# Turning h and K through DRAM in a two-layer graph kernel: h's blocks by two stores and eight fetches, K's by one store and four, with a rearranged loop, start and end

## The chip, the cores and the metric

The kernel runs on one core of one Trainium2 chip (trn2). The metric is the device time of one execution in microseconds (us). The kernel before took 1233.65 us in the median of 3 runs (1232.67 to 1234.98). All tensors are float32.

## The reference, cut to what is computed

x is 128 matrices of 128 rows (graph nodes) by 512 features; adj is one 128x128 matrix of zeros and ones with a full diagonal. Each of the 128 matrices is worked on alone.

```python
h = relu(layernorm(x))
z_l, z_g, v = h @ W_lang.T, h @ W_grav.T, h @ W_V.T
zn = z_l / norm(z_l)                        # row norms
A_l = max(zn @ zn.T, 0) * not_eye           # 128 x 128
d2  = max(sq + sq.T - 2 * z_g @ z_g.T, 0)
A_g = exp(-d2 / (2 * sigma**2)) * not_eye
K = w_l * row_normalised(A_l * adj) + (1 - w_l) * row_normalised(A_g * adj)
x = x + (K @ v) @ W_O.T                     # layer 0
h = relu(layernorm(x))
x = x + (adj * adj).T @ h + bias            # layer 1
```

## The kernel before, in words

**Tiles.** Four matrices (GB) form a group, and 32 groups (NG) pass through a software pipeline of 32 iterations. A slot of `x_ring` holds one group's x, [128 rows, 4 matrices, 512]. float32 products are made of three passes of a split pair (`passes`, line 183): every operand X is kept as X_hi (a copy by ACT, rounded to the PE's format) and X_lo = X - X_hi (by DVE, `lo`, line 586). So each result in PSUM costs an ACT copy and then a DVE subtraction before the bank is free.

**Weights folded at the start.** W_lang and W_grav are squared into lower block triangles `Lw`, W_V and W_O into `MT`. Then h Lw h^T gives one triangle's half of a symmetric matrix, called P here, and P + P^T is the full one. The turn of P, a transpose of [128,128] per matrix, is made of a DVE transpose of 32x32 blocks (`turn_p`, line 775) and transfers that move the blocks across partitions through DRAM (`store_p` 223, `fetch_p` 227). `sum_s` (line 784) adds P and its turned form.

**One iteration i on PE** (line 978): eight `y_block` products of group i (60 matmuls of 512 columns) into the ring of five PSUM banks; the 96 matmuls of 256 columns into `p_ps` (line 998), with the four transposes of K of group i-1 between them (`transposes_K`, line 954, into `kt_ps`); `k_v` of group i-1 for four matrices (12 matmuls); the product v of group i (48 matmuls); `layer1` of group i-2 (12 matmuls). PE takes a ring bank only when `drained` has counted its last reader (`free`, line 931).

**The others.** ACT (line 433) copies y_hi, h2_hi, K^T_hi (`kt_copy`, 527, from `kt_ps`), P, v_hi, and hT_hi of the next group out of `h_turned` (`turned_hi`, 427), and computes exponentials, norms' outputs and h2. DVE (line 702) makes the lo parts, statistics, masks, `combine` (the last step of K), residual sums (`add` 658, `output` 689), and turns the 32x32 blocks of h in place (`turn_blocks`, 602). POOL makes h2_lo, adds the bias, and computes in this order: the factors of the second layernorm of group i-1 (`norm2`, 336, which needs all four `stats` of DVE), `row_norms` of i (345), `norm1` of i+2, `mask_norms` of i.

**SP's queue** (line 249) takes all transfers in a written order: load x of i+2, the 16 transfers of `turn_h` (243) that move each 32x32 block column of h to its partitions within SBUF, then P's first store, the store of the row norms (it waits for POOL's `row_norms`), P's second store, four fetches, the spread of the norms, four fetches, four stores of the output.

**Order that matters below.** On DVE: ... y_lo 5, y_lo 6, `combine`, blocks of h, y_lo 7, y_lo 8, blocks of h, `kt_lo`, four x statistics, then adds and statistics of group i-1 with the last `stats` before most of the squared norms of i, then v_lo, hT_lo and `turn_p`. On ACT: `kt_copy` before the two copies of P; then per matrix b: v_hi, hT_hi, with h2 of matrix 0 (`h2_full`, 494) placed behind hT_hi of b = 2, ahead of v_hi of b = 3. PE's next `y_block` waits for all four hT_lo (line 980).

Of the kernel before, what the change touches and what calls it, by code (L numbers as in the profile page):

```python
# [5 lines left out]
ALU = mybir.AluOpType  # L6
# [14 lines left out]
def gnn_pair(nc, x, adj, w_lang, w_grav, w_v, w_o, gate_logit, log_sigma, bias, out):  # L21
# [12 lines left out]
    TURN = 16 * NQ * NQ  # L34
    assert C == NQ

# [19 lines left out]
    with ExitStack() as ctx:  # L56
# [65 lines left out]

        p_dram = [nc.dram_tensor(f"p_dram_{l}", [P, NQ, GB * Q], F32).ap() for l in range(2)]
# [47 lines left out]
        blocks_ready, turned = sem("blocks_ready"), sem("turned")  # L171
        p_blocks = sem("p_blocks")
        p_stored, p_turned = [[sem(f"p_{what}_{l}") for l in range(2)] for what in ("stored", "turned")]
        ht_hi, ht_lo = sem("ht_hi"), sem("ht_lo")
        ln2_last = sem("ln2_last")
# [4 lines left out]
        x2b_last = sem("x2b_last")  # L180
# [14 lines left out]
        def h_blocks(i, j):  # L195
            return h[i * Q:(i + 1) * Q, j].rearrange("p b c q -> p (b c q)")

        def turned_to(i, j):
            return h_turned[j * Q:(j + 1) * Q, i].rearrange("p b c q -> p (b c q)")
# [3 lines left out]

        def x_rows(g, b):

            return x_ring[:, bass.ds(g % SLOTS, 1), b].rearrange("p s d -> p (s d)")

# [4 lines left out]
        def _(sp):  # L212
# [3 lines left out]

            def store_out(g, use):
                for b in range(GB):
                    sp.wait_ge(drained, use + b + 1)
                    sp.dma_start(out_g[bass.ds(g, 1), b].rearrange("g n d -> (g n) d"),  # L220
                                 x_rows(g, b)).then_inc(out_stored, 16)
# [21 lines left out]
            def turn_h(g):  # L243
                sp.wait_ge(blocks_ready, GB * g)
                for i in range(NQ):
                    for j in range(NQ):
                        sp.dma_start(turned_to(i, j), h_blocks(i, j)).then_inc(turned, 16)  # L247
# [33 lines left out]
            iteration(NG - 2, load=False)  # L281
            use = first_use(NG - 1) + PER - GB
            store_out(NG - 3, use)
            store_out(NG - 2, use + 2 * GB)
            store_out(NG - 1, use + 3 * GB)
# [4 lines left out]
        def _(pool):  # L290
# [61 lines left out]
            def iteration(i, before=True, lag=True, after=True, x_next=True):  # L352
# [10 lines left out]
                if before and not after:  # L363
# [14 lines left out]
            for b in range(GB):  # L378
                h2_lo(NG - 2, b)
            g = NG - 1  # L380

            def last_factors(q):
# [3 lines left out]
                pool.tensor_tensor(ln2[:, RSTD, b0:b1], ln2[:, VAR, b0:b1], neg_half[:, b0:b1], ALU.pow)\  # L386
                    .then_inc(ln2_rstd, 1)
                pool.wait_ge(ln2_rstd, 2 * q + 1)
                pool.tensor_tensor(ln2[:, SHIFT, b0:b1], ln2[:, NEG_MEAN, b0:b1], ln2[:, RSTD, b0:b1], ALU.mult)\
# [3 lines left out]
            for b in range(GB // 2):  # L393
                add_bias(g, b)
            last_factors(1)
            for b in range(GB // 2, GB):
                add_bias(g, b)


        @block.scalar  # L400
        def _(act):
# [5 lines left out]
            def normalize(g, b0):  # L407
                if b0 == 0:
# [3 lines left out]
                    elif not isinstance(g, int) or g > 1:  # L412
                        act.wait_ge(turned, TURN * (g - 1))
# [13 lines left out]
            def turned_hi(g, b):  # L427
                if b == 0:
                    act.wait_ge(turned, TURN * g)
# [3 lines left out]
            def iteration(i, before=True, lag=True, after=True):  # L433
# [30 lines left out]
                if not after:  # L464
                    shift(i)
                for c in range(C):
                    if not before:
                        act.wait_ge(setup_mm, 3 * C + c + 1)
                        act.activation(MT[0][:, c], bank(n), ACT.Copy).then_inc(hi_ready, 1)
                    n += 1  # L470
                if before:
                    act.wait_ge(kv_done, GB * i)
                for b in range(GB):
                    if not after and b == 1:
                        exponentials(i)
                    act.wait_ge(v_done, GB * i + b + 1)
                    act.activation(v[0][:, b], bank(n), ACT.Copy).then_inc(hi_ready, 1)  # L477
                    n += 1
                    if after:
                        turned_hi(i + 1, b)  # L480
                    if not after and b == GB - 2:
# [3 lines left out]
                    if before and after:  # L485
                        for k in {0: [], 1: [], 2: [0], 3: [1, 2, 3]}[b]:
# [7 lines left out]
            def h2_full(g, b, last=False):  # L494
# [4 lines left out]
                if b == 0:  # L499
                    wait_for(act, h2_split, GB * g)  # L500
                act.activation(h2f[:, b], x_rows(g, b), ACT.Relu, bias=ln2[:, SHIFT, b:b + 1],  # L501
                               scale=ln2[:, RSTD, b:b + 1]).then_inc(h2_done, 1)

            def h2_copy(g, b):
                act.wait_ge(h2_done, GB * g + b + 1)
                if b == 0:
# [13 lines left out]
            def w_g_K_g(g):  # L520
                act.wait_ge(deg_step, 5 * g + 5)
                wait_for(act, kt_done, g)
# [4 lines left out]
            def kt_copy(g):  # L527
                act.wait_ge(kt_done, g + 1)
                wait_for(act, kv_done, GB * g)
                act.activation(KT[0][:, :, :], kt_ps[:, :, :], ACT.Copy).then_inc(kt_hi, 1)  # L530
# [32 lines left out]
            lw_hi(1, side, side_hi, 2, C)  # L563
            for b in range(GB):
                t_hi(b, SETUP + b)
            act.wait_ge(a2_step, 1)
# [9 lines left out]
            for b in range(GB):  # L576
                h2_full(NG - 1, b, last=True)
                h2_copy(NG - 1, b)
# [3 lines left out]
        def _(dve):  # L582
# [70 lines left out]

            def kt_lo(g):
                dve.wait_ge(kt_hi, g + 1)
                dve.tensor_tensor(KT[1][:, :, :], kt_ps[:, :, :], part(KT[0][:, :, :]), ALU.subtract).then_inc(kt_split, 1)
# [8 lines left out]
            def last_factors(b0, b1, before):  # L665

                t = [ln2[:, n, b0:b1] for n in range(LN_STEPS)]
                m0, m1, q0, q1 = (bn2[:, b0:b1, n] for n in (1, 4, 2, 5))
# [435 lines left out]
```

## Time and profile before

| | |
|---|---|
| median of 3 runs | 1233.65 us (1232.67 to 1234.98) |
| the profiled execution, and its span | 1233.85 us, span 1232.1 us |
| mean granted TensorE clock | 0.992 |
| PE / DVE / ACT / POOL busy | 97% / 86% / 58% / 50% |
| chain that ended last | PE 93%, DVE 3%, ACT 1%, SP's queue 1% |
| DMA | mean 118 GB/s; SP's queue 38% of 16 engines |

```profile
PE   7989999999999999999999999999999999999994
DVE  5667888899888889888888988888898888899878
PEclk9999999999999999999999999999999999999998
h_turned<-h SPq DMA_DIRECT2D x496, 64.0 KB, 2.0
```

Each digit is the busy share of one fortieth of the span (30.8 us) in tenths; PEclk is the granted clock likewise. A matmul record ends where a model puts it, so starts are the safer numbers. A line such as "x496, 64.0 KB, 2.0" is a kind of transfer, its count, its size and the median us from issue to landing.

### The profile page before, as it was taken

How to read it: one execution, taken by the hardware profiler on the slowest of the kernel's cores; microseconds unless marked ns; L12 is line 12 of the kernel's file. 1: busy time of each engine (PE TensorE's matmuls, PEld its weight loads, DVE VectorE, ACT ScalarE, POOL GpSimd, SP SyncE). 2: the span in 40 equal slices, each digit the busy share in tenths (PEclk: the TensorE clock that was granted, in tenths of full speed). 3: DMA queues.
4: the chain of work that ended last, by engine and by line, in shares of the span. 5: the costliest groups of instructions: out<-in, count | busy, mean ns of one | idle time of the engine just before them, and what ended most of it. 6: DMA issues, size and time to landing. Idle time of an engine off the chain costs nothing.

```text
span 1232.1 us, 22833 instructions
## 1 busy us (share of the span) xinstructions
PE 1199.0 (97%) x6076; PEld 1023.3 (83%) x6076; DVE 1062.1 (86%) x1892; ACT 714.5 (58%) x1324; POOL 610.9 (50%) x991
## 2 busy tenths in 40 slices
PE   7989999999999999999999999999999999999994
PEld 7777888888888888888888888888888888888882
DVE  5667888899888889888888988888898888899878
ACT  5344655665565566556566655556665555665543
POOL 1203554545655444665454466545456554545545
PEclk9999999999999999999999999999999999999998
DMA  7122234344333444433343443344443334443302
GB/s 267 52 77 77 75 113 136 127 128 145 111 96 118 140 128 132 138 117 95 120 136 128 136 121 118 102 126 133 127 141 113 108 112 135 129 126 111 111 1 103
DMA packets 115457, 145.10 MB, mean 118 GB/s; under 512 B 20848, under 2 KB 52720, under 8 KB 115440
## 3 DMA queue, kind: packets, MB, share of 16 engines
q1 hardware_dynamic: 114864, 144.57, 38.4%
q10 hardware_dynamic: 576, 0.33, 0.1%
q8 instruction: 7, 0.11, 0.0%
q14 instruction: 10, 0.08, 0.0%
HBM read 62.46 MB, written 49.87 MB: 91 GB/s over the span
## 4 chain that ended last, share of the span: by engine, by line
PE 93%; DVE 3%; ACT 1%; SPq 1%; issue 1%; DMA 0%; POOL 0%; DVEq 0%; POOLq 0%
PE ring L944 76%; PE p_ps L998 14%; PE kt_ps L957 1%; PE ring L1042 1%; SPq L247 1%; DMA x_ring<-in_L_gnn_W_lang 0%; ACT h2f L501 0%; DVE bn L663 0%; DVE x_ring L698 0%; ACT h L419 0%; DVE chain L802 0%; PE ring L1051 0%; DVE v_lo L589 0%; DVE x_ring L660 0%; DVE ln L676 0%
## 5 line engine op out<-in xcount | busy, mean ns | idle before, releaser
L342 POOL TENSOR_TENSOR h_lo<-h2f,h_hi 128x512 fp32r<-128x512 f32 x124 | 156.7, 1292 | 323.3 <-ACT h_hi L508 323.1
L944 PE MATMUL ring<-hT_hi,Lw_hi 128*128 128x512 f32 x640 | 250.5, 391 | 7.5 <-DVE hT_lo L609 4.3
L944 PE MATMUL ring<-hT_hi,Lw_lo 128*128 128x512 f32 x640 | 250.4, 391 | 0.0
L944 PE MATMUL ring<-hT_lo,Lw_hi 128*128 128x512 f32 x640 | 250.4, 391 | 0.0
L589 DVE TENSOR_TENSOR y_lo<-ring,y_hi 128x512 fp32r<-128x512 f32 x256 | 169.7, 682 | 46.8 <-ACT y_hi L440 46.5
L944 PE MATMUL ring<-MT_hi,hT_hi 128*128 128x512 f32 x512 | 199.4, 389 | 1.4 <-DVE MT_lo L589 1.4
L944 PE MATMUL ring<-MT_hi,hT_lo 128*128 128x512 f32 x512 | 199.2, 389 | 0.0
L944 PE MATMUL ring<-MT_lo,hT_hi 128*128 128x512 f32 x512 | 199.2, 389 | 0.0
L440 ACT ACTIVATE y_hi<-ring 128x512 fp32r<-128x512 f32 x256 | 152.2, 597 | 79.1 <-PE ring L944 75.1
L477 ACT ACTIVATE v_hi<-ring 128x512 fp32r<-128x512 f32 x128 | 76.0, 594 | 190.1 <-PE ring L944 190.1
L327 POOL TENSOR_TENSOR x_ring<-x_ring,bias_sb 128x512 f32 (+1 forms) x124 | 157.8, 1304 | 1.9 <-ACT h2f L501 1.9
L944 PEld LDWEIGHTS ring<-hT_hi,Lw_hi 128*128 128x128 f32 x640 | 121.0, 189 | 34.1 <-DVE h_lo L870 2.8
L998 PE MATMUL p_ps<-y_hi,hT_hi 128*128 128x256 f32 x512 | 147.1, 287 | 0.0
L998 PE MATMUL p_ps<-y_hi,hT_lo 128*128 128x256 f32 x512 | 145.0, 283 | 0.0
L998 PE MATMUL p_ps<-y_lo,hT_hi 128*128 128x256 f32 x512 | 144.9, 283 | 0.0
L944 PEld LDWEIGHTS ring<-hT_hi,Lw_lo 128*128 128x128 f32 x640 | 120.9, 189 | 25.2
L944 PEld LDWEIGHTS ring<-hT_lo,Lw_hi 128*128 128x128 f32 x640 | 120.8, 189 | 25.2
L944 PEld LDWEIGHTS ring<-MT_hi,hT_hi 128*128 128x128 f32 x512 | 96.1, 188 | 21.7 <-DVE MT_lo L589 1.8
L944 PEld LDWEIGHTS ring<-MT_hi,hT_lo 128*128 128x128 f32 x512 | 96.1, 188 | 20.0
L944 PEld LDWEIGHTS ring<-MT_lo,hT_hi 128*128 128x128 f32 x512 | 96.1, 188 | 19.9
L431 ACT ACTIVATE hT_hi<-h_turned 128x512 fp32r<-128x512 f32 x124 | 77.6, 625 | 55.3 <-DMA h_turned<-h 55.3
L333 POOL TENSOR_TENSOR chain<-rn_cols,mask 128x512 f32<-128x512 f32 x31 | 48.3, 1558 | 122.2 <-DMA rn_cols<-rn_dram 122.2
(163 smaller groups left out, 2536.1 us busy)
## 6 DMA issues: line engine op xcount, KB each, us to landing
x_ring<-in_x SPq DMA_DIRECT2D x32, 1024.0 KB, 5.3
out<-x_ring SPq DMA_DIRECT2D x128, 256.0 KB, 2.6
h_turned<-h SPq DMA_DIRECT2D x496, 64.0 KB, 2.0
p_dram<-chain SPq DMA_DIRECT2D x62, 256.0 KB, 2.5
h<-p_dram SPq DMA_DIRECT2D x248, 64.0 KB, 2.6
rn_cols<-rn_dram SPq DMA_DIRECT2D x31, 256.0 KB, 4.0
x_ring<-in_L_gnn_W_lang SPq DMA_DIRECT2D x4, 256.0 KB, 5.2
h2f<-in_L_gnn_W_grav SPq DMA_DIRECT2D x1, 1024.0 KB, 8.9
```

The costliest lines, as they stand in the source:

```text
L247: sp.dma_start(turned_to(i, j), h_blocks(i, j)).then_inc(turned, 16)
L327: pool.tensor_tensor(x_rows(g, b), x_rows(g, b), bias_sb[:, :], ALU.add).then_inc(x2b_ready, 1)
L333: pool.tensor_tensor(rn_mask, rn_cols[:, :, :].rearrange("p m b -> p b m"), by_row, ALU.mult)\
L342: pool.tensor_tensor(h2[1][:, b], h2f[:, b], h2[0][:, b].bitcast(F32), ALU.subtract)\
L431: act.activation(hT_columns(0, b), h_columns(b), ACT.Copy).then_inc(ht_hi, 1)
L440: act.activation(y[0][:, a, :, l], bank(n).rearrange("p (b m) -> p b m", b=GB), ACT.Copy)\
L477: act.activation(v[0][:, b], bank(n), ACT.Copy).then_inc(hi_ready, 1)
L589: return dve.tensor_tensor(out, ps, part(hi), ALU.subtract)
L944: mm = pe.matmul(out, lhsT, rhs, start=(k == 0), stop=(k == len(terms) - 1))
L957: mm = pe.transpose(kt_ps[:, b], K[:, b], ident[:, :])
L998: mm = pe.matmul(p_ps[:, b].rearrange("p l m -> p (l m)"), lhsT, rhs, start=(a == 0 and k == 0 and b % 2 == 0), stop=(a == C - 1 and k == ...
L1042: mm = pe.matmul(bank(c)[:, 0:D - c * P], lhsT, rhs, start=(e == 0 and k == 0), stop=(e == C - 1 and k == 2))
```

## The change

- **h.** DVE still turns 32x32 blocks in place. In place of 16 transfers in SBUF, each half of the group (two matrices) is stored to DRAM by one transfer of 512 KB and brought back by four of 128 KB; ACT's `turned_hi` waits for its half only.
- **K.** PE's four transposes of K leave every iteration but the last. DVE gets `turn_K` (behind `combine`), SP one store of 256 KB and four fetches of 64 KB, and `kt_copy`/`kt_lo` read K from SBUF instead of PSUM.
- **Order in the loop.** PE makes the first v before the four `k_v`. ACT makes `kt_copy` behind the copies of P. DVE goes from the x statistics to the squared norms of i, with `kt_lo` among them, then v_lo 0, then the adds and statistics of i-1; hT_lo 0 stands before the last `stats`.
- **Start.** The hi/lo splits of the folded weights are spread over the first iteration's y products, h's transposed copies come earlier, the first v waits for MT column by column, and in the first two iterations hT of the last matrix comes before its v.
- **End.** In the last iteration `layer1` of group 29 is moved behind everything else, into other PSUM; the bias of the last two groups is added by PE (two more matmuls for each output); the last norm has buffers of its own, so it no longer waits for the one before; POOL's bias adds for the last groups vanish.

SP's new order and the loops' core:

```diff
+            def store_h(g, l):
+                sp.wait_ge(blocks_ready, GB * (g - 1) + (l + 1) * HALF)
+                sp.dma_start(h_dram[l], h_half(h, l)).then_inc(h_stored[l], 16)
+            def fetch_h(g, l):
+                sp.wait_ge(h_stored[l], 16 * g)
+                for j in range(NQ):
+                    sp.dma_start(h_half(h_turned, l)[j * Q:(j + 1) * Q],
+                                 h_dram[l][:, j].rearrange("(i r) e -> r i e", r=Q)).then_inc(turned[l], 16)
+            def store_K(g):
+                sp.wait_ge(k_blocks, g + 1)
+                sp.dma_start(k_dram, K_blocks.rearrange("p j b q -> p j (b q)")).then_inc(k_stored, 16)
+            def fetch_K(g):
+                sp.wait_ge(k_stored, 16 * g + 16)
+                for j in range(NQ):
+                    sp.dma_start(K_turned[j * Q:(j + 1) * Q].rearrange("r i b q -> r i (b q)"),
+                                 k_dram[:, j].rearrange("(i r) e -> r i e", r=Q)).then_inc(k_turned, 16)
             def iteration(i, load=True, lag=True):
...
-                turn_h(i + 1)
+                if before:
+                    store_K(i - 1)
+                store_h(i + 1, 0)
+                if before:
+                    fetch_K(i - 1)
+                store_h(i + 1, 1)
+                fetch_h(i + 1, 0)
+                fetch_h(i + 1, 1)
                 spread_norms_turn_p(i)
```

```diff
 # ACT
                 if before:
-                    kt_copy(i - 1)
                     act.wait_ge(s_ready, 2 * i)
                 for half in range(2):
                     act.wait_ge(p_done, GB * i + 2 * half + 2)
...
+                if before:
+                    kt_copy(i - 1)
 # DVE
+            def turn_K(g):
+                dve.wait_ge(k_ready, g + 1)
+                dve.wait_ge(p_stored[1], 16 * g + 16)
+                dve.transpose(K_blocks.rearrange("p j b q -> p b j q"),
+                              K[:, :, :].rearrange("p b (j q) -> p b j q", q=Q)).then_inc(k_blocks, 1)
...
                             combine(i - 1)
+                            turn_K(i - 1)
...
-                    if before:
-                        kt_lo(i - 1)
...
                 if before:
-                    add(i - 1, 0, n)
...
                     diagonal(i, 0)
+                    kt_lo(i - 1)
                     squares(i, 0)
                     diagonal(i, 1)
                     squares(i, 1)
+                    v_lo(0)
+                    add(i - 1, 0, n + 1)
+                    add(i - 1, 1, n + 2)
+                    dve.wait_ge(drained, use + n + 3)
...
+                    add(i - 1, 2, n + 3)
+                    stats(i - 1, 0)
+                    stats(i - 1, 1)
...
+                    add(i - 1, 3, n + 4)
+                    stats(i - 1, 2)
...
+                    turned_lo(i + 1, 0)
+                    stats(i - 1, 3)
 # PE
-                    if before and a == 1:
-                        transposes_K(i - 1)
-                if before:
-                    pe.wait_ge(kt_split, i)
...
                     mm.then_inc(v_done, 1)
+                    if before and b == 0:
+                        pe.wait_ge(kt_split, i)
+                        for kb in range(GB):
+                            k_v(i - 1, kb, n + 1 + kb, use + n + 1 + kb)
```

The end of DVE's part:

```diff
-            last_residual(g, first_use(NG))
+            last_residual(g, first_use(NG) - GB)
             for b in range(GB):
-                output_bias(g - 1, b, GB + b)
-            h2_lo(g, 0)
-            for b in range(1, GB):
+                late_output(g - 2, b)
+            for b in range(GB):
                 h2_lo(g, b)
-                output(g, b - 1, 2 * GB + b - 1)
-            output(g, GB - 1, 3 * GB - 1)
+                late_output(g - 1, b)
+            for b in range(GB):
+                late_output(g, b)
```

## Rows read from the trace of the kernel before

**Rows 1.** Chain that ended last, middle of the run: start us, us, what
```profile
240.87 0.44 PE kt_ps L957 x4
...
563.20 2.87 PE p_ps L998 x24
...
569.39 29.95 PE ring L944 x132
599.33 2.87 PE p_ps L998 x24
```
**Rows 2.** Timeline of DVE in one iteration: start, us, engine line op [idle before]
```profile
567.87 2.46 DVE L600 BATCH_NORM_STATS2 bn<-x_ring 128x6 f32 x4
570.28 1.32 DVE L660 TENSOR_TENSOR x_ring<-ring,x_ring 128x512 f32 x2
571.94 0.69 DVE L660 TENSOR_TENSOR x_ring<-ring,x_ring 128x512 f32 x1 [0.33 <-DVE x_ring L660]
...
575.52 0.69 DVE L663 BATCH_NORM_STATS2 bn<-x_ring 128x6 f32 x1
...
576.71 0.68 DVE L802 TENSOR_TENSOR chain<-chain,diag_of 128x512 f32<-128x512 f32 x1
...
584.29 0.68 DVE L609 TENSOR_TENSOR hT_lo<-h_turned,hT_hi 128x512 fp32r<-128x512 f32 x1
```
**Rows 3.** Timelines of ACT and, last line, of POOL, same iteration
```profile
568.70 1.32 ACT L462 ACTIVATE chain<-p_ps 128x512 f32<-128x512 f32 x2 [1.48 <-PE p_ps L998]
...
583.05 0.60 ACT L477 ACTIVATE v_hi<-ring 128x512 fp32r<-128x512 f32 x1 [0.90 <-PE ring L944]
584.07 2.22 ACT L501 ACTIVATE h2f<-x_ring,ln 128x512 f32 x3
...
579.67 0.20 POOL L319 TENSOR_TENSOR ln<-ln 128x4 f32<-128x4 f32 x1
```
**Rows 4.** Timeline of SP's queue, same iteration: issues
```profile
580.87 0.33 SPq L236 DMA_DIRECT2D rn_dram<-rn  x1
581.97 0.32 SPq L225 DMA_DIRECT2D p_dram<-chain  x1
...
584.81 1.77 SPq L230 DMA_DIRECT2D h<-p_dram  x4
```
**Rows 5.** Timeline of DVE, the following iteration: first sum and `combine`
```profile
589.73 1.28 DVE L787 TENSOR_TENSOR chain<-h,chain 128x512 f32<-128x512 f32 x2
...
596.43 1.14 DVE L650 SCALAR_TENSOR_TENSOR K<-chain,deg,K 128x128 f32<-128x128 f32 x4
```
**Rows 6.** P's stores (line 225), then P's fetches (line 230), whole run
```profile
DMA to landing us min/median/max: 2.0/2.5/3.0
...
DMA to landing us min/median/max: 1.9/2.6/4.5
```
**Rows 7.** Waits of PE over the whole run: total, times, longest us
```profile
PE ring L944 <- DVE h_lo L687: 10.0, 1, 10.0
...
PE ring L944 <- DVE hT_lo L609: 4.3, 2, 2.2
PE ring L944 <- DVE h_lo L870: 2.4, 1, 2.4
...
PE p_ps L1026 <- ACT chain L513: 1.5, 1, 1.5
```
**Rows 8.** Chain that ended last, first iterations
```profile
78.23 13.89 PE ring L944 x60
...
114.08 15.52 PE ring L944 x60
```
**Rows 9.** Timeline of DVE: `kt_lo` in iteration 2
```profile
133.66 0.69 DVE L656 TENSOR_TENSOR KT_lo<-kt_ps,KT_hi 128x512 fp32r<-128x512 f32 x1 [1.49 <-ACT KT_hi L530]
```
**Rows 10.** Stretch 114.5:130: us, busy by engine, granted clock, DMA share, GB/s
```profile
114.50:130.00 15.50, 15.50 (x65) 12.71 (x64) 11.26 (x22) 9.94 (x18) 1.53 (x1) 0.89 0.16 41
```
**Rows 11.** Page, costliest groups: POOL's h2_lo
```profile
L342 POOL TENSOR_TENSOR h_lo<-h2f,h_hi 128x512 fp32r<-128x512 f32 x124 | 156.7, 1292 | 323.3 <-ACT h_hi L508 323.1
```

More of the change, by code:

```diff
@@ L170, in gnn_pair @@
         h2_split_dve = sem("h2_split_dve")
-        blocks_ready, turned = sem("blocks_ready"), sem("turned")
+        blocks_ready = sem("blocks_ready")
+        h_stored, turned = [[sem(f"h_{what}_{l}") for l in range(2)] for what in ("stored", "turned")]
         p_blocks = sem("p_blocks")
@@ L362, in iteration @@
                     norm1(i + 2)
-                if before and not after:
+                if not after:
+                    pool.wait_ge(bias_hi, 2)
+                    pool.tensor_tensor(bias_parts[1], bias_sb[:, :], bias_parts[0].bitcast(F32), ALU.subtract)\
+                        .then_inc(bias_split, 1)
                     norm2(i - 1)
@@ L412, in normalize @@
                     elif not isinstance(g, int) or g > 1:
-                        act.wait_ge(turned, TURN * (g - 1))
+                        for l in range(2):
+                            act.wait_ge(turned[l], 16 * NQ * (g - 1))
                         act.wait_ge(s_ready, 2 * g - 2)
@@ L475, in iteration @@
                         exponentials(i)
+                    if not lag and b == GB - 1:
+                        turned_hi(i + 1, b)
                     act.wait_ge(v_done, GB * i + b + 1)
-                    act.activation(v[0][:, b], bank(n), ACT.Copy).then_inc(hi_ready, 1)
-                    n += 1
-                    if after:
+                    if before and b == 0:
+                        act.wait_ge(kv_done, GB * (i - 1) + 1)
+                    act.activation(v[0][:, b], bank(n + v_use(b, before)), ACT.Copy).then_inc(hi_ready, 1)
+                    if after and (lag or b < GB - 1):
                         turned_hi(i + 1, b)
-                    if not after and b == GB - 2:
+                    if not after and b == 1:
                         w_g_K_g(i)
@@ L709, in iteration @@
                         lo(y[1][:, a, :, l], bank(n).rearrange("p (b m) -> p b m", b=GB), y[0][:, a, :, l], hi)\
-                            .then_inc(drained, 1)
+                            .then_inc(drained, 1 if lag or n < G_USES - 1 else 1 + GB)
                         n += 1
-                        if not before and n == 1:
-                            for q in range(C):
+                        if not before:
+                            for q in {1: [C], 2: [C + 1], 3: [C + 2, C + 3], 4: [0, 1], 5: [2], 6: [3]}.get(n, []):
                                 factor_lo(q)
-                        if not before and 2 <= n <= 3:
-                            factor_lo(C + 2 * n - 4)
-                            factor_lo(C + 2 * n - 3)
                         if before and n == 3:
@@ L962, in k_v, with layer1, late_layer1 @@
                 product(bank(n), passes([w[:, b] for w in KT], [w[:, b] for w in v])).then_inc(kv_done, 1)
-            def layer1(g, b, n, use, last=False):
-                if last:
+            def layer1(g, b, n, use):
+                pe.wait_ge(h2_split, GB * g + b + 1)
+                free(use)
+                product(bank(n), passes([w[:, :] for w in A2], [w[:, b] for w in h2])).then_inc(l1_done, 1)
+            def late_layer1(g, b, ps):
+                if g == NG - 1:
                     pe.wait_ge(h2_split_dve, b + 1)
@@ L984, in iteration @@
                         n += 1
[L985 to L986 removed]
+                        if not before and n == 2:
+                            transposes_w_o(C // 2)
+                            transposes_w_o(C // 2 + 1)
                         if not before and n == BANKS - 1:
@@ L1002, in iteration @@
                             mm.then_inc(p_done, 1)
-                    if before and a == 1:
-                        transposes_K(i - 1)
-                if before:
-                    pe.wait_ge(kt_split, i)
-                    for b in range(GB):
-                        k_v(i - 1, b, n + b, use + n + b)
-                else:
+                if not lag:
+                    n += GB
+                if not before:
                     pe.wait_ge(w_split, 3 * C)
@@ L1071, in _ @@
             g = NG - 1
-            use = first_use(NG)
+            use = first_use(NG - 1)
+            n = LAST_FIRST
             pe.wait_ge(kt_split, NG)
             for b in range(GB):
-                k_v(g, b, b, use + b)
-            for b in range(GB):
-                layer1(g - 1, b, GB + b, use + GB + b)
-            for b in range(GB):
-                layer1(g, b, 2 * GB + b, use + 2 * GB + b, last=True)
+                if b == GB - 1:
+                    pe.wait_ge(drained, use + n)
+                k_v(g, b, n + b, use + n + b)
+            n += GB
+            free(use + n)
+            late_layer1(g - 2, 0, bank(n))
+            for b in range(1, GB):
+                late_layer1(g - 2, b, late[b - 1])
+            pe.wait_ge(bias_split, 1)
+            for l1_g, b in LAST_OUTPUTS:
+                n += 1
+                free(use + n)
+                late_layer1(l1_g, b, bank(n))
 _INS = ["x", "adj", "L0_gnn_W_lang", "L0_gnn_W_grav", "L0_gnn_W_V", "L0_gnn_W_O",
```

268 lines of the change are left out of this document (152 added, 116 removed).

## The prediction, with its working

> **What bounds the kernel now.** I read the chain that ended last first: 93% of it is PE. In the middle of the run it repeats without a gap: P's products, K's four transposes, then 132 matmuls in 29.95 us, 0.227 us each [rows 1]. From 563.20 to 599.33 is one iteration, 36.13 us: y products 60 x 0.227 = 13.6, P's 5.75 (569.39 - 563.20 less the 0.44 of the transposes), `k_v` 2.7, v 10.9, `layer1` 2.7. PE's waits, read next, are few and lie in the first three and in the last iterations [rows 7]. So three things can move the time: PE's own work, the waits at both ends, and whether the other engines still keep up once PE's work shrinks and their order changes. The last needs the timelines of DVE, ACT, POOL and SP in one iteration, read as loops: how long from one event until the same event of the next group, through everything that must happen between.
>
> **PE's own work.** Four transposes at 0.44 us [rows 1] leave 31 iterations: 13.6 us if nothing else gets late; the period would be 35.70. h's new transfers cost PE nothing: I take their landing some 4 us before hT_hi wants them, as two stores and eight issues at 0.44 us [rows 4] replace 16 issues that took 10 us of SP's queue.
>
> **Loop A, from `kt_lo` to `kt_lo` through the second layernorm.** Count from the start of `kt_lo` = 0. In the new order DVE must do 14 instructions until the last `stats` of group i-1 begins. Ten at 0.60 apart (four statistics begin 567.87, the next instruction 570.28), two whose result the next one reads at 0.7 (their own 0.68 and a little), a tiny one at 0.10, and 1.06 from the second add to the third (570.28 + 0.60 to 571.94): 8.6 [rows 2]. Today the last `stats` begins 12.3 us behind the start of P's products (575.52 - 563.20) [rows 1, 2]; in the new order `kt_lo` itself begins 6.95 behind it (below), so it is 15.5. That is what the new order costs: `stats` is three us later, and `norm2` waits for it. From its start to the end of `norm2` is 4.35 (575.52 to 579.87) [rows 2, 3]: 12.95. ACT, in its written order, does h2 of matrix 0 there (0.74) [rows 3] before v_hi 3, which PE had ready over a us before: v_hi 3 begins at 13.7, hT_lo 3 1.24 later (583.05 to 584.29), and PE's next y products 0.8 behind that: 15.75 [rows 2, 3]. Then 13.6 of y and 0.1 for a restarted PE: P's products begin at 29.45. The second P copy began today when they ended (the first at 568.70, 5.50 behind 563.20, of which 0.44 goes) [rows 1, 3]: it begins at 5.78 behind, `kt_copy` 0.5 later, `kt_lo` 0.65 after that, so 6.95. Loop A = 29.45 + 6.95 = **36.4**. PE then waits some 0.7 us in every iteration for hT_lo.
>
> **Loop B, through P's and K's transfers.** The same 8.6. From `stats`' start until the row norms are stored 5.35 (to 580.87), because `row_norms` stands behind `norm2` on POOL: 13.95. P's second store is an issue later, 14.4; its fetches begin 2.84 behind it (581.97 to 584.81), the fourth 1.35 later, 18.6 [rows 4]; it lands in 2.45: 21.05 [rows 6]. From the sum's start to `combine`'s start 6.70, to its end 7.84 [rows 5]: 28.95. `turn_K`, a transpose like `turn_p`, 0.75: 29.7. K's store: 2.0 at least, 3.0 at most, 2.5 median [rows 6]; I take 2.1, since nothing else is in flight behind it at first: 31.85. The last of four fetches is issued 1.35 later and lands in 2.5 (bounds 1.9 and 4.5 [rows 6]; h's first store of 512 KB stands ahead of it by 1 us): 35.7. Copy and wake-up 0.7: **36.4**, from 35.8 with the shortest landings to 37.3 with a store of 2.5 and a fetch of 3.0. SP waits in `fetch_K` with h's second store and all of h's fetches queued behind it; h lands by 11.5 us behind the start of P's products and is wanted after 9.8 (first half, landed by 8.5) and 17, so nobody is late for that.
>
> The Trainium skill, "DMA: Bandwidth & Descriptors", section "Anatomy of one DMA — SWDGE (gpsimd) path", fits a DMA as 2.0 us plus its bytes at 436 GB/s; 256 KB would take 2.6 us there. The trace agrees with its size for the median store and not for the shortest [rows 6]. By that figure for K's store loop B would be 36.9 and the time near 1240; the sum does not use it.
>
> **Loop C, DVE alone**: `combine`'s start (27.8) to the next `kt_lo`: `turn_K`, four block transposes, two y_lo, four statistics, `diagonal`, 13 steps at 0.60 and 0.6 of dependence: 36.2. Close, not the bound.
>
> Three loops within 0.2 us, so the period is 36.4, 0.27 more than now. Over 29 periods: +7.8.
>
> **The start.** Today iteration 1's y begin at 78.23 and iteration 2's at 114.08, each behind a wait of about 2.1 [rows 7, 8]; the second took 15.52 instead of 13.89 at a granted clock of 0.89 [rows 8, 10]. Another wait and slow stretch lie in iteration 0. In the new order W_O's factors come right behind y_lo, so that wait goes (2.4 [rows 7], and I estimate 1.6 of slow clock behind it, as behind 114.08); h's copies are 0.5 earlier; the first v does not wait for the last MT column (1.4); hT_hi 3 before v_hi 3 gives 0.6. I get iteration 1's y at 71.9 and its `kt_lo` at 92.5, and from there one round of loop B (no x in it that could shorten it): `kt_lo` of iteration 2 at 128.5 instead of 133.66 [rows 9]. **-5.2**, give or take 1.5. PE is further ahead than that, but the loops take it back.
>
> **The end.** From `kt_lo` of the last iteration, 133.66 + 29 x 36.13 = 1181.4 [rows 1, 9], the end now takes 50.7 us, with 10.0 in which PE waits for the last h2_lo [rows 7]. New: P turned by PE at 4 to 5, sum, masks and K by 14.5, K turned and split 16.6, `k_v` to 19.6; DVE's adds, `stats` and two sets of factors to 27.9; POOL's power and product 29.8, two h2_lo at 1.29 [rows 11] to 32.4 (they stand behind the factors, and ACT needs their buffer); h2, its copy, DVE's lo, five matmuls, the last output: 37.5; store and finish 2.7: 40.2. **-10.5**, give or take 3. The 16 bias matmuls cost 0.23 each; all but the last two lie under ACT's and POOL's steps, and those two are in the 37.5.
>
> **Sum.** Span 1232.1 - 5.2 + 7.8 - 10.5 = 1224.2. Check: 128.5 + 29 x 36.4 + 40.2 = 1224.3. The profiled execution took 1233.85 for a span of 1232.1, 1.75 more, and lies within 0.2 us of the median of the runs. Forecast **1226 us**.
>
> **Rivals.**
> - *PE stays the bound.* If my counted loops are too long by 0.7 (DVE's third add may not wait, `norm2` may be quicker without its neighbours), the period is 35.70. Against it: three loops, each summed from starts in one iteration. P's products of iteration 2 begin at 120.1; 120.1 + 29 x 35.70 + 6.95 + 40.2 + 1.75 = 1204 us.
> - *K's trip through DRAM takes PE's place.* K^T came 0.4 us after `combine` could be read by PE; now it takes a block transpose, a store, four fetches. For it: the store may take 2.5 to 3.0 and the fetch has seen 4.5 [rows 6]; h's 512 KB lie in front. With K's last block 0.7 later, loop B = 37.1: 128.5 + 1075.9 + 40.2 + 1.75 = 1246 us, slower. It decides from a period of 36.67: there gains at the ends are eaten.
> - *The clock.* A wait in each iteration could drop the clock as after the 2.16 us wait at 114.08 [rows 8, 10]. Against it: waits of 0.7 are shorter than the one of 1.5 us before P's last transposes [rows 7], and there the chain shows no slow stretch behind it. At 1.6 us for each it would be 1270.
> - *The turn of h was the bound and is relieved.* PE's waits name hT_lo twice only, in the start; in the middle nothing waits for it on PE [rows 7]. It gives nothing beyond the start.
>
> **Chances.** Period 36.2 to 36.57 (1220 to 1231): 0.50. Period 35.7 to 36.2, with the first rival (1204 to 1220): 0.17. 36.57 to 36.75, where it comes out level: 0.10. K's trip longer still: 0.20, the clock 0.03. The range of 8 in 10 is 1207 to 1243: it leaves out the lowest part of the first rival and the far part of the second. A measurement of this kernel tells about 0.2% (2.5 us) from no change; faster 0.67, within it 0.10, slower 0.23.
>
> **What would show it.** PE waits of 0.5 to 0.9 us for hT_lo before the y products of nearly every iteration; `kt_copy` at 6.3 behind the start of P's products, by P's copies or by K's landing; POOL's `norm2` starting 16.2 behind it instead of 13.1; ACT's v_hi 3 held by h2 0; DVE idle before the first sum by a us; a period of 36.4; the end 10 us shorter. A wait of PE for KT_lo in every iteration speaks for the second rival, none at all for the first. What would make it wrong: a landing or a handful of DVE steps mis-sized by 0.3 us, since it is paid 29 times (9 us).

## The result and the profile after

The changed kernel takes 1310.44 us in the median of 4 runs (1309.76 to 1311.04) beside 1233.34 for the kernel before: a ratio of 1.062, 95% interval 1.0605 to 1.0641. It is 77 us slower, where 1226 us had been forecast and 1243 was the upper end of the range. Its profiled execution has a span of 1309.3 us at a granted clock of 0.997.

The page's busy times:

```profile
PE 1211.5 (93%) x5968; PEld 1004.8 (77%) x5968; DVE 1135.8 (87%) x1919; ACT 702.8 (54%) x1326; POOL 636.1 (49%) x988
```

PE's waits over the whole run, as total, times and longest us (against [rows 7]):

```profile
PE ring L1027 <- DVE hT_lo L680: 36.1, 30, 1.5
PE ring L1027 <- DVE KT_lo L737: 29.6, 29, 1.5
PE ring L1118 <- DVE v_lo L660: 11.0, 29, 0.4
```

Where PE had no wait in the middle, it now has three in every iteration, 2.6 us together in this list. So a loop of other engines sets the period (a chain of steps that leads from one group's event to the next group's same event), and the place to read is one iteration of DVE, from `kt_lo` to `kt_lo` (start, us, what; the first lines answer to [rows 2, 9], the later ones to [rows 5]):

```profile
561.66 1.64 DVE L737 TENSOR_TENSOR KT_lo<-K,KT_hi 128x512 fp32r<-128x512 f32 x1
563.22 0.67 DVE L897 TENSOR_REDUCE sq<-chain 128x4 f32<-128x512 f32 x1
563.82 1.17 DVE L890 TENSOR_TENSOR chain<-chain,diag_of 128x512 f32<-128x512 f32 x1
...
565.74 0.43 DVE L900 TENSOR_SCALAR sqc<-sq 128x4 f32<-128x4 f32 x1
...
571.88 0.68 DVE L744 BATCH_NORM_STATS2 bn<-x_ring 128x6 f32 x1
...
584.93 1.95 DVE L874 TENSOR_TENSOR chain<-h,chain 128x512 f32<-128x512 f32 x2 [1.35 <-DMA h<-p_dram]
...
592.30 1.14 DVE L721 SCALAR_TENSOR_TENSOR K<-chain,deg,K 128x128 f32<-128x128 f32 x4
...
600.92 1.63 DVE L737 TENSOR_TENSOR KT_lo<-K,KT_hi 128x512 fp32r<-128x512 f32 x1
```

POOL, ACT and SP's queue in the same iteration:

```profile
561.02 6.37 POOL L383 TENSOR_TENSOR x_ring<-x_ring,bias_sb 128x512 f32 x4
576.08 0.20 POOL L375 TENSOR_TENSOR ln<-ln 128x4 f32<-128x4 f32 x1
584.19 1.55 POOL L389 TENSOR_TENSOR chain<-rn_cols,mask 128x512 f32<-128x512 f32 x1 [2.91 <-DMA rn_cols<-rn_dram]
...
600.26 0.63 ACT L601 ACTIVATE KT_hi<-K 128x512 fp32r<-128x512 f32 x1 [0.77 <-DMA K<-k_dram]
...
577.27 0.34 SPq L262 DMA_DIRECT2D rn_dram<-rn  x1
580.61 1.79 SPq L256 DMA_DIRECT2D h<-p_dram  x4
594.32 0.34 SPq L281 DMA_DIRECT2D k_dram<-chain  x1
596.34 2.34 SPq L286 DMA_DIRECT2D K<-k_dram  x4
```

The period is 600.92 - 561.66 = 39.26 us here, against 36.4 forecast and 36.13 before [rows 1]. ACT's copy of K, behind the landing of K's last block, ends at 600.89, and DVE's work before `kt_lo` ends at 600.86, so at this point K's trip and DVE's own queue of work are level. Two things stand out. First, `kt_lo` (L737) takes 1.64 us; before it took 0.69 [rows 9]. Second, the DVE steps that are long, L737 and the second L890, lie beside POOL's four bias adds (561.02 to 567.39), and the 1.95 us of the two sums lie beside POOL's L389. In the kernel before, the four adds lay elsewhere:

```profile
569.45 5.04 POOL L327 TENSOR_TENSOR x_ring<-x_ring,bias_sb 128x512 f32 x4
```

From 569.45 to 574.49 DVE did statistics and residual adds [rows 2], which read at most one tensor from SBUF; `diagonal` began at 574.93, just behind. One line for a whole run shows the first (min/median/max of one, ns; first and last start):

```profile
L737 DVE TENSOR_TENSOR KT_lo<-K,KT_hi x31: 693/1573/1673, 92.2 to 1265.2; 128x512 fp32r<-128x512 f32 x31
```

In the kernel before the same group reads 691/692/692. POOL pays as well: one of its bias adds takes 1623 ns in the mean where it took 1293. `diagonal` takes 943 where it took 702. These are the groups of before and of after (busy us, mean ns):

```profile
L327 POOL TENSOR_TENSOR x_ring<-x_ring,bias_sb 128x512 f32 x112 | 141.2, 1293 | 0.0
L802 DVE TENSOR_TENSOR chain<-chain,diag_of 128x512 f32<-128x512 f32 x64 | 44.9, 702 | 0.8 <-ACT chain L462 0.8
```

```profile
L383 POOL TENSOR_TENSOR x_ring<-x_ring,bias_sb 128x512 f32 x112 | 178.5, 1623 | 0.0
L890 DVE TENSOR_TENSOR chain<-chain,diag_of 128x512 f32<-128x512 f32 x64 | 60.4, 943 | 5.1 <-ACT chain L518 5.0
```

**Theory**, to be tested below. A DVE instruction that reads two tensors from SBUF cannot run beside a POOL instruction that reads SBUF: one waits for the other, and its record shows the wait as duration. `kt_lo` used to read `kt_ps`, in PSUM; the change made it read K from SBUF, and the new order put it and `diagonal` under POOL's bias adds, at the head of both counted loops. **Rivals**: h's way through DRAM; K's way through DRAM with its landings; the new order as such, with `norm2` behind the squared norms.

### The profile page after: what moved, and what is told of

Same layout as the page of the kernel before. It is cut to its first block, busy times and chain, and to the rows that moved or that the text cites. A ratio compares the mean times of both kernels' runs of the same rounds, so it can differ in the third digit from the quotient of the medians.

```text
span 1309.3 us, 22837 instructions
## 1 busy us (share of the span) xinstructions
PE 1211.5 (93%) x5968; PEld 1004.8 (77%) x5968; DVE 1135.8 (87%) x1919; ACT 702.8 (54%) x1326; POOL 636.1 (49%) x988
## 4 chain that ended last, share of the span: by engine, by line
issue 47%; POOL 37%; PE 6%; DVE 5%; DMA 2%; POOLq 2%; ACT 1%; SPq 0%; DVEq 0%; ACTq 0%
POOL x_ring L383 14%; POOL h_lo L398 7%; POOL ln L373 5%; PE ring L1027 3%; POOL rn L404 2%; POOL ln L367 2%; POOL ln L366 2%; PE ring L1118 1%; POOL ln L371 1%; POOL ln L365 1%; PE p_ps L1096 1%; POOL ln L362 1%; PE ring L1145 1%; POOL ln L369 1%; POOL ln L363 1%
## 5 line engine op out<-in xcount | busy, mean ns | idle before, releaser
L1027 PE MATMUL ring<-hT_hi,Lw_hi 128*128 128x512 f32 x640 | 252.6, 395 | 38.8 <-DVE hT_lo L680 36.1
L1118 PE MATMUL ring<-MT_hi,hT_hi 128*128 128x512 f32 x512 | 203.2, 397 | 11.0 <-DVE v_lo L660 11.0
L383 POOL TENSOR_TENSOR x_ring<-x_ring,bias_sb 128x512 f32 (+1 forms) x120 | 190.8, 1619 | 0.0
L660 DVE TENSOR_TENSOR y_lo<-ring,y_hi 128x512 fp32r<-128x512 f32 x256 | 166.5, 680 | 15.0 <-ACT y_hi L497 14.9
L497 ACT ACTIVATE y_hi<-ring 128x512 fp32r<-128x512 f32 x256 | 146.9, 587 | 30.3 <-PE ring L1027 29.3
L566 ACT ACTIVATE h2f<-x_ring,ln 128x512 f32 (+1 forms) x128 | 97.3, 806 | 84.7 <-POOL ln L375 84.7
L660 DVE TENSOR_TENSOR v_lo<-ring,v_hi 128x512 fp32r<-128x512 f32 x128 | 85.6, 669 | 52.5 <-ACT v_hi L540 52.5
L361 POOL TENSOR_TENSOR ln<-bn 128x4 f32<-128x4 f32 x63 | 13.0, 206 | 210.2 <-DVE bn L744 191.5
```

What stands on the lines that cost most here:

```text
L383: pool.tensor_tensor(x_rows(g, b), x_rows(g, b), bias_sb[:, :], ALU.add).then_inc(x2b_ready, 1)
L497: act.activation(y[0][:, a, :, l], bank(n).rearrange("p (b m) -> p b m", b=GB), ACT.Copy)\
L566: act.activation(h2f[:, b], x_rows(g, b), ACT.Relu, bias=ln[:, SHIFT, b:b + 1], scale=ln[:, RSTD, b:b + 1]).then_inc(h2_done, 1)
L660: return dve.tensor_tensor(out, ps, part(hi), ALU.subtract)
L1027: mm = pe.matmul(out, lhsT, rhs, start=(k == 0), stop=(k == len(terms) - 1))
L1118: mm = pe.matmul(bank(m), lhsT, rhs, start=(c == 0 and k == 0), stop=(c == C - 1 and k == len(terms) - 1))
```

## The experiments

Each is timed beside the kernel before, which took 1231.55 to 1233.25 us in these sessions. The ratio is to it.

**h's way alone** (`h_only`): the kernel before with the two stores and eight fetches of h, and nothing else.

```diff
-                turn_h(i + 1)
+                store_h(i + 1, 0)
+                store_h(i + 1, 1)
+                fetch_h(i + 1, 0)
+                fetch_h(i + 1, 1)
```

> The kernel before with h's turned blocks through DRAM (two stores, eight fetches), and nothing else of the change. Theory (two loops through DVE's new order, POOL and SP, and DVE steps stretched by POOL): h's way is not in them, so 1228 to 1234 us, the period stays at 36.13 us, a little less at the start because SP issues for 5 us instead of 10. Rival 'traffic' (the 48 MB more that now cross DRAM slow every transfer, P's among them): P's fetches land later than 2.5 us and the time is over 1240 us.

Measured: 1233.55 us, ratio 1.0012 (1.0003 to 1.0022), and PE's waits are those of [rows 7] within 0.1 us. h's way costs 0.12% at this place, next to nothing, and gains nothing by itself.

**K by PE again** (`pe_K`): the kernel after, with PE's four transposes into `kt_ps` in every iteration and no K in DRAM, so that `kt_lo` reads PSUM.

```diff
-                    act.wait_ge(k_turned, 16 * NQ * (g + 1))
-                    act.activation(KT_columns(0), K_turned, ACT.Copy).then_inc(kt_hi, 1)
+                act.wait_ge(kt_done, g + 1)
+                act.activation(KT[0][:, :, :], kt_ps[:, :, :], ACT.Copy).then_inc(kt_hi, 1)
```

> The changed kernel with K turned by PE into PSUM again, all else as changed (order, h, start, end). Theory: kt_lo reads PSUM again and takes 0.69 us instead of 1.6, and K's trip is out of the loop; the loop over the second layernorm and h2 of matrix 0 remains: 9.2 to the last stats, 7.3 to y, 13.7 to P's products, 7.4 to kt_lo: a period of 37.6 us, so 1255 to 1270 us. Rival 'K's trip alone': the period falls to 36.1 and the time to about 1220 us. Rival 'traffic': over 1290 us.

Measured: 1270.48 us, ratio 1.0312 (1.0295 to 1.0329). Of PE's waits of every iteration only that for hT_lo is left, 35.0 us in 30. `kt_lo`, in the same place beside the same POOL instructions:

```profile
L723 DVE TENSOR_TENSOR KT_lo<-kt_ps,KT_hi x32: 677/678/691, 93.3 to 1244.5; 128x512 fp32r<-128x512 f32 x32
```

With one operand in PSUM it is not lengthened. The time is half a us above the expected range. K's way is worth some 38 of the 77 us here, by its transfers, `turn_K` and `kt_lo` together; without it the kernel is still 39 us slower than before. That rest is not the order alone: in the iteration looked at, the first `diagonal` (both inputs in SBUF), which now meets POOL's last h2_lo and first bias add, takes 1.53 us.

**POOL's bias adds cut to one column** (`no_bias`). The bias is left out of all but the first column of these groups' outputs; the count of instructions and every wait stay.

```diff
-                pool.tensor_tensor(x_rows(g, b), x_rows(g, b), bias_sb[:, :], ALU.add).then_inc(x2b_ready, 1)
+                pool.tensor_tensor(x_rows(g, b)[:, 0:1], x_rows(g, b)[:, 0:1], bias_sb[:, 0:1], ALU.add)\
+                    .then_inc(x2b_ready, 1)
```

> The changed kernel with POOL's four bias adds in each iteration cut to one column, so nearly all of the bias is left out for the groups that POOL adds it to; order and waits stay. Theory: kt_lo falls from 1.6 us to 0.69 and the second diagonal from 1.2 to 0.68, 1.45 us less in each of 30 periods: 1262 to 1270 us. Rival 'order alone' (the new order costs it all, the long kt_lo is hidden): within 5 us of 1310. Rival 'traffic': the same.

Measured: 1271.77 us, ratio 1.0330 (1.0312 to 1.0347). The line of `kt_lo` for the whole run:

```profile
L738 DVE TENSOR_TENSOR KT_lo<-K,KT_hi x31: 691/693/727, 92.9 to 1225.7; 128x512 fp32r<-128x512 f32 x31
```

DVE's timeline in one iteration, with the two steps and the last `stats` that the loops count to:

```profile
584.17 0.69 DVE L738 TENSOR_TENSOR KT_lo<-K,KT_hi 128x512 fp32r<-128x512 f32 x1 [0.19 <-ACT KT_hi L602]
585.37 0.68 DVE L891 TENSOR_TENSOR chain<-chain,diag_of 128x512 f32<-128x512 f32 x1
592.70 0.69 DVE L745 BATCH_NORM_STATS2 bn<-x_ring 128x6 f32 x1
```

Same instruction, same operands, same place; only its neighbour is gone, and it takes 0.69 us. From `kt_lo` to the last `stats` it is now 8.53 us, as the prediction counted (8.6). That is 37 us of the 77 by the distance to the kernel before beside each, 39 by the two times; the time is 1.8 us above the expected range. The mean period stays at (1225.7 - 92.9)/30 = 37.76, so something else is late as well. In this iteration the first sum begins at 605.62, `combine` at 612.78 and the next `kt_lo` at 621.74. So from the last `stats` to the sum it is 12.92 us where the prediction counted 12.45, from there to `combine` 7.16 where it counted 6.70 (the sums still lie beside POOL's `mask_norms`), and K's trip is 8.96 where it counted 8.65: `kt_lo` now waits for K's copy by 0.41.

**The order on POOL and ACT.** Both loops begin with the same DVE front and then pass through POOL, one behind `norm2` to ACT's h2, one through `norm2` to `row_norms`. `rows_first` lets POOL do `row_norms` before `norm2`:

```diff
+                row_norms(i)
                 if before and after:
                     norm2(i - 1)
-                row_norms(i)
```

`h2_late` moves ACT's h2 of matrix 0 behind hT_hi 3, so that v_hi 3 does not stand behind it:

```diff
-                        for k in ({0: [], 1: [], 2: [0], 3: [1, 2, 3]} if lag else {0: [], 1: [], 2: [], 3: [0, 1, 2, 3]})[b]:
+                        for k in {0: [], 1: [], 2: [], 3: [0, 1, 2, 3]}[b]:
```

and `rows_h2` does both.

> The changed kernel with only POOL's move: row_norms before norm2. Theory: the loop over the row norms' store and P's second half binds today at 39.1 us, and the loop over norm2 and h2 of matrix 0 lies close below, at about 38.2 (10.2 to the last stats, 7.3 to y, 13.7 to P's products, 7.0 to kt_lo). So this alone brings the period to 38.2 and the time to about 1280 us (1272 to 1288). Rival 'only one loop is real' (that over the row norms): the same as with both moves, 1242 us.

> The changed kernel with only ACT's move: h2 of matrix 0 behind hT_hi of matrix 3. Theory: the loop over the row norms stays at 39.1 us and only PE's wait moves, from hT_lo to KT_lo: 1300 to 1311 us. Rival 'only the loop over h2 is real': 1242 us.

> The changed kernel with two moves: POOL makes row_norms before norm2, and ACT makes h2 of matrix 0 behind hT_hi of matrix 3. All the work and all the transfers stay. Theory: both loops are cut, the one over the row norms' store and P's second half by 2.8 us to about 36.4, the one over h2 0 to what PE allows: period 36.3 to 36.9, so 1222 to 1242 us. Rival 'traffic' or 'DVE is simply full' (1136 us busy of 1309): over 1280 us, since neither move changes the traffic or DVE's work.

Measured: `rows_first` 1285.12 us, 1.0420 (1.0399 to 1.0441); `h2_late` 1314.17 us, 1.0656 (1.0634 to 1.0678); `rows_h2` 1242.46 us, 1.0089 (1.0073 to 1.0106). `rows_first` alone brings 25 us, `h2_late` alone nothing (4 us slower, 3 above its expected range; its interval overlaps that of the changed kernel), both together bring 68. That is how two loops that start from one point behave: relieving one leaves the other. The waits name which: PE waits for hT_lo (36.0 us in 30) in `rows_first`, for KT_lo (44.4 in 30) in `h2_late`. In `rows_h2` the wait for hT_lo is gone and that for KT_lo is down to 5.2 us in 29, and DVE has no idle between `combine` and `combine` except 0.37 us for y_hi and 0.33 for a result of its own:

```profile
560.24 1.15 DVE L721 SCALAR_TENSOR_TENSOR K<-chain,deg,K 128x128 f32<-128x128 f32 x4
568.27 1.14 DVE L890 TENSOR_TENSOR chain<-chain,diag_of 128x512 f32<-128x512 f32 x1
569.51 1.60 DVE L737 TENSOR_TENSOR KT_lo<-K,KT_hi 128x512 fp32r<-128x512 f32 x1
571.63 1.18 DVE L890 TENSOR_TENSOR chain<-chain,diag_of 128x512 f32<-128x512 f32 x1
...
597.14 1.14 DVE L721 SCALAR_TENSOR_TENSOR K<-chain,deg,K 128x128 f32<-128x128 f32 x4
```

Its period is DVE's own 36.90. Some 2.5 us of it are what `kt_lo`, the two `diagonal` and the two sums take above their 0.69, 0.68, 0.68 and 1.28 (1.60, 1.14, 1.18 and 1.91).

**Both moves, K by PE** (`pe_K_rows_h2`).

> The changed kernel with K turned by PE and both moves: h through DRAM, the new start and end, the new order with its loops cut. Theory: PE's own 36.14 us is the period again (no long kt_lo, no turn_K on DVE), so 29 periods as before and the gains at both ends remain: start 4 to 9, end 6 to 10, so 1214 to 1224 us. Rival 'DVE is full anyway': 1235 us or more, with DVE busy without a gap over the period.

Measured: 1230.16 us, 0.9976 (0.9967 to 0.9986): better than before by 0.24%, and 6 us short of what was expected. PE is never idle in the middle by the records, yet the period is 36.4, not 36.13. The chain shows where (start, us, what):

```profile
600.55 2.75 PE ring L1105 x12
603.29 2.72 PE ring L1012 x12
606.01 8.45 PE ring L1105 x36
```

The 36 matmuls of the last three v take 8.45 us instead of 36 x 0.227 = 8.17. One iteration earlier the first of them starts at 569.59, and `v_lo` of matrix 0, which frees its bank, ends at 569.54 (568.86 + 0.68): a wait for the bank, too short for the list of waits.

**`v_lo` 0 earlier** (`v_first`): `pe_K_rows_h2` with one line moved.

```diff
                     diagonal(i, 1)
+                    v_lo(0)
                     squares(i, 1)
-                    v_lo(0)
```

> pe_K_rows_h2 with v_lo 0 moved ahead of the second squares on DVE. There the second v product of PE began at 569.59, right when v_lo 0 had ended (569.54), 0.23 later than the matmuls before it led to expect. Theory (this wait for the ring bank is the missing 0.24 us of each period, too short to stand in the list of waits): the period falls from 36.37 to 36.13, 1230.2 - 29 x 0.24 = 1223 us, between 1221 and 1225, and the chain shows 8.17 us for the 36 matmuls instead of 8.43. Rival (the pause belongs to the place of k_v between two v products, whatever DVE does): it stays within 2 us of 1230.

Measured: 1242.58 us, 1.0082 (1.0064 to 1.0101). The bank wait is gone as expected, the 36 matmuls take 8.16 us in two of the periods looked at, and yet the kernel is 12 us slower, where neither the theory nor its rival had put it: PE now waits 14.1 us in 29 for hT_lo. DVE's front got longer against POOL:

```profile
572.31 1.69 DVE L875 TENSOR_TENSOR chain<-chain,diag_of 128x512 f32<-128x512 f32 x1
...
575.36 1.07 DVE L885 TENSOR_SCALAR sqc<-sq 128x4 f32<-128x4 f32 x1
```

The second `diagonal` takes 1.69 us where it took 1.25 in `pe_K_rows_h2`, and the tiny L885, which took 0.42 there and 0.17 in `no_bias`, takes 1.07. The wait was found rightly; that moving it was free was not.

**`kt_lo` on POOL.** If POOL makes `kt_lo` itself, between its h2_lo and its bias adds, DVE loses its longest collision.

```diff
 # POOL
+            def kt_lo(g):
+                pool.wait_ge(kt_hi, g + 1)
+                pool.tensor_tensor(KT_columns(1), K_turned, KT_columns(0).bitcast(F32), ALU.subtract)\
+                    .then_inc(kt_split, 1)
...
+                if before:
+                    kt_lo(i - 1)
                 if lag:
 # DVE
                     diagonal(i, 0)
-                    kt_lo(i - 1)
```

`kt_pool_only` is the kernel after with this edit, `kt_pool` is `rows_h2` with it.

> The kernel after, in which POOL makes kt_lo between its h2_lo and its bias adds; nothing else is moved. In the kernel after, kt_lo holds DVE for 1.56 us (561.66 to 563.22) at the head of both loops. Theory (both loops begin with DVE's front, and what it does there counts in full in each iteration): the front is 1.56 us shorter, so is the period (39.1 to 37.55): 1310.4 - 29 x 1.56 = 1265 us, between 1260 and 1272; PE waits for hT_lo as before, for KT_lo hardly. Rival (kt_lo costs DVE 0.60 as everywhere else and the rest of the stretch has another cause): 1310.4 - 29 x 0.60 = 1293 us. If a loop that does not pass DVE's front sets the period, it stays above 1300.

> The changed kernel with both moves, K through DRAM as changed, and kt_lo made by POOL ahead of its bias adds instead of by DVE beside them. Theory: with both moves DVE itself bound at 36.8 us, of which kt_lo was 1.6; without it PE's 35.70 is the bound: period 35.7 to 36.0, time 1200 to 1215 us. Rival 'K's trip through DRAM binds': PE waits for KT_lo in each iteration and the time stays over 1230 us.

Measured: `kt_pool_only` 1283.20 us, 1.0409 (1.0392 to 1.0427); `kt_pool` 1214.65 us, 0.9847 (0.9831 to 0.9864). The first lies between the two theories: 27 us gained, not 45 nor 17. DVE's front lost the 1.56 us, but the mean period fell by 0.98 only (39.14 to 38.16). The second `diagonal`, beside POOL's `kt_lo`, takes 1.36 instead of 1.17, and PE still waits 30.2 us in 30 for KT_lo; what holds back the rest was not isolated. The second is clearly faster than both kernels: 28 us from the same edit once the order lets both loops go.

**`kt_copy` between P's two copies** (`kt_mid`), in `kt_pool`:

```diff
                     act.activation(P_sb[:, 2 * half:2 * half + 2], p_ps[:, 2 * half:2 * half + 2], ACT.Copy)\
                        .then_inc(p_copied, 1)
-                if before:
-                    kt_copy(i - 1)
+                    if before and half == 0:
+                        kt_copy(i - 1)
```

> kt_pool with ACT's kt_copy placed between the two copies of P. In kt_pool kt_copy stood behind both (594.61), POOL's kt_lo waited 0.70 us for it, and PE's k_v began 0.17 us late behind kt_lo. K has landed by about 594. Theory: KT_lo comes about 0.6 us earlier, k_v no longer waits, the period falls from 35.9 to 35.73: 1214.65 - 29 x 0.17 = 1210 us, between 1208 and 1212. Rival (the second copy of P, now 0.6 us later, delays the second diagonal and with it the statistics or P's trip until PE waits for them): 1214 us or more.

Measured: 1208.32 us, **0.9799 (0.9783 to 0.9815)**. The period, read from ACT's first copy of P, is 35.74:

```profile
590.36 0.60 ACT L526 ACTIVATE chain<-p_ps 128x512 f32<-128x512 f32 x1 [2.36 <-PE p_ps L1102]
...
626.10 0.60 ACT L526 ACTIVATE chain<-p_ps 128x512 f32<-128x512 f32 x1 [2.36 <-PE p_ps L1102]
```

That is the prediction's floor for PE, 35.70, reached: h and K through DRAM, four transposes an iteration off PE, and 2.0% faster than before. So the transfers were no obstacle; the neighbours of DVE's instructions and the places in the order were.

## Why the prediction was wrong, point by point

**PE's own work, h's way**: right in what they cost PE. h's way alone is neutral, and with the loops out of the way the period is 35.74 against 35.70 counted. Wrong is the landing of h some 4 us before hT_hi wants it: ACT waits for it 17.3 us in 30 in the changed kernel, since eight fetches are issued in 4.65 us and land in 3.3. In the iteration shown this held nobody, because DVE's hT_lo 0 stands 5 us behind hT_hi 0 (571.28 and 565.57).

**The start**: right in the first iteration (`kt_lo` at 92.2, 92.5 predicted), 1.7 us late in the second (130.16 against 128.5), since one slow round of the loop lies between.

**Loops A and B**: the failed step. All loops were found, and it was seen that they nearly tie; but each DVE step was priced at 0.60, 0.7 or 1.28, from rows in which POOL held up none of them, and the overlap of these steps with POOL's was taken to cost nothing. Loop B by its own terms, the iteration shown above against the prediction's count:

| stretch | predicted | measured | difference |
|---|---|---|---|
| `kt_lo` to last `stats` | 8.6 | 561.66 to 571.88: 10.22 | +1.62 |
| to the row norms' store | 5.35 | to 577.27: 5.39 | +0.04 |
| to the first sum (fetch issued and landed) | 7.1 | to 584.93: 7.66 | +0.56 |
| to `combine` | 6.70 | to 592.30: 7.37 | +0.67 |
| `combine`, K through DRAM, to `kt_lo` | 8.65 | to 600.92: 8.62 | -0.03 |
| period | 36.4 | 39.26 | +2.86 |

The first term is POOL's bias adds: `kt_lo` holds DVE for 1.56 instead of 0.60 (+0.96), the second `diagonal` 1.20 instead of 0.7, L900 0.35 instead of 0.10. `no_bias` removes just these and gives 8.53. The fourth is the two sums, 1.95 instead of 1.28 [rows 5], beside POOL's `mask_norms`; that POOL is the cause there rests on the same pattern and was not tried alone. The third is a transfer: 3.0 us from the issue of the last of four fetches (581.96) to the sum instead of 2.45; it is within the bounds that the prediction had read [rows 6] and had not used at their far end. K's trip, the rival it feared most, came out to 0.03 us: its store landed in 2.0 us in the median of 31, near the 2.1 of the sum and not the 2.6 of the other figure, and its fetches in 2.2. Loop C is level with it, as said above.

Per period +2.74 in the mean ((1265.2 - 130.16)/29 = 39.14), times 29, is +79.4 us; the second iteration +1.7, the end +3.9. Together 85.0, and the span is 1309.3 - 1224.2 = 85.1 above the sum.

**The rival of K's trip through DRAM** had the right sign and place (PE waits for KT_lo in every iteration) and the wrong mechanism and size: it priced a longer landing at 0.7 us a period and the whole at 1246 us. None of the rivals named a DVE instruction that gets longer. The trace of before held it, in its last iteration, where POOL's bias adds happen to lie over `diagonal`:

```profile
1183.70 5.93 POOL L327 TENSOR_TENSOR x_ring<-x_ring,bias_sb 128x512 f32<-128x512 f32 x4
...
1184.99 1.79 DVE L802 TENSOR_TENSOR chain<-chain,diag_of 128x512 f32<-128x512 f32 x1
1187.42 1.06 DVE L802 TENSOR_TENSOR chain<-chain,diag_of 128x512 f32<-128x512 f32 x1
```

The same line takes 0.68 in [rows 2]. Its spread over the run, 671/680/1790 ns, would have shown it; the prediction took one instance. Two small slips of its sums change nothing: by its own numbers loop B with the shortest landings is 35.7 (not 35.8), and the clock rival 1272 us (not 1270).

**The end**: 44.1 us from the last `kt_lo` (1309.3 - 1265.2), against 40.2 predicted and 50.7 before. The saving is there, smaller by 3.9, and again beside POOL. These are DVE's steps of the last norm, on two columns each, first free and then under POOL's h2_lo, and the lo part of h2:

```profile
1288.92 0.16 DVE L751 TENSOR_TENSOR ln<-bn 128x2 f32<-128x2 f32 x1
1289.18 0.16 DVE L755 SCALAR_TENSOR_TENSOR ln<-ln 128x2 f32<-128x2 f32 x1
...
1292.31 2.65 POOL L398 TENSOR_TENSOR h_lo<-h2f,h_hi 128x512 fp32r<-128x512 f32 x2 [1.47 <-ACT h_hi L575]
...
1292.47 1.13 DVE L751 TENSOR_TENSOR ln<-bn 128x2 f32<-128x2 f32 x1
1293.70 1.28 DVE L755 SCALAR_TENSOR_TENSOR ln<-ln 128x2 f32<-128x2 f32 x1
1298.06 1.41 DVE L766 TENSOR_TENSOR h_lo<-h2f,h_hi 128x512 fp32r<-128x512 f32 x1
```

0.97 + 1.12 + 0.73 us over their free durations (0.16, 0.16, 0.68), and about 1 more in the front of that iteration. The last norm of the kernel before shows the same on the same step (1.26 us, at 1210.07), so its trace had this too.

**The signs to look for**: PE's wait for hT_lo was to be 0.5 to 0.9 us and is 1.2 (36.1 in 30); a wait for KT_lo in every iteration was named as the sign of the second rival and is there, 1.0 each. What they left out is that both loops could be long at once, from the front that they share.

## What to carry to other kernels

Before an instruction of DVE is moved, or one of its operands is moved from PSUM to SBUF, look at what POOL does at its new place: price it from a row with such a neighbour, and read min, median and max of its group, not one instance. When loops tie, list what they share and what each has alone; relieve the shared part first, or each one's own part together, and don't judge one such move by itself. A faster order may only show once the last of several collisions is gone: the same two routes through DRAM are 6% slower or 2% faster than before, by three places in the order and the engine of one subtraction.

## What the runs showed of the hardware

A DVE `tensor_tensor` of 128x512 with both inputs in SBUF takes 0.69 us alone and 1.57 in the median beside POOL's adds (`kt_lo`), one of 128x2 takes 0.16 alone and 1.13 beside a POOL instruction of 1.3: the added time (0.9 and 1.0 us, for 512 columns and for 2) does not grow with the work and stays below one POOL instruction. So it is a wait, not a slower stream. The two long steps of the last norm end at 1293.60 and 1294.98; POOL's two h2_lo beside them run from 1292.31 to 1294.96, so that the first of them ends near 1293.6. The same subtraction with one input in PSUM takes 0.68 beside the same adds, and DVE's reductions (0.67) and 32x32 transposes (1.28 for two, beside POOL's h2_lo) are not touched. POOL's add rises from 1.29 to 1.62.

The Trainium skill, "SBUF — State Buffer", section "Who interferes with whom", has this rule: a DVE instruction with two inputs in SBUF contends with a GpSimd (POOL) instruction that reads SBUF, over a pair of ports that only one of them can hold at a time, and a reduction does not contend. The traces agree: `kt_lo` takes 693 ns in the median without the neighbour, 1573 with it, and the reduction 0.67 us beside it. It should have been a rival in the prediction, since the diff turns `kt_lo`'s first operand from `kt_ps` into K in SBUF.

A `tensor_scalar` on 128x4 with one SBUF input (L900) was lengthened too, 0.43 instead of 0.17. The same section says that such an instruction can take the shared pair, in a mode that uses both ports, if its operands meet the conditions; the trace does not show the mode.

One wait stayed invisible in the list of waits: in `pe_K_rows_h2`, a bank that came free some 0.25 us late hides under the modelled end of the matmul before it. The spacing of PE's starts (0.34 instead of 0.227) or the chain's sums show it.
